# A graph network on one core: four small jobs move between VectorE, GpSimd and other places of their own queues

## The reference

```
h = relu(layernorm(x))
agg = segment_sum(h[src], dst)                      # layer 0: sums over edges
t = relu(batch_norm(((1 + eps) * h + agg) @ W1 + b1))
x = x + h + relu(batch_norm(t @ W2 + b2))

h = relu(layernorm(x))                              # layer 1: messages over edges
m = mish(mish([h[src], h[dst], edge_attr] @ W1 + b1) @ W2 + b2)
agg = segment_sum(m, dst)
u = mish([h, agg] @ W3 + b3)
y = h + u @ W4 + b4
x = x + layernorm(y) * gamma + beta
```

## Time and profile before

| quantity | value |
|---|---|
| time, median of 3 runs | 1142.65 us (1142.56 to 1143.2) |
| time of the profiled execution | 1142.65 us |
| its span, first to last instruction | 1140.8 us |
| mean granted TensorE clock | 0.953 |
| TensorE matmuls busy | 1061.1 us (93%) |
| VectorE, ScalarE, GpSimd busy | 875.8, 898.0, 676.5 us |
| chain that ended last | TensorE 85%, VectorE 10% |

### The profile page before, as it was taken

The page is one execution under the profiler, slowest core; times in us unless marked ns, Lnnn a source line. Parts: engine busy times, 40 slices in busy tenths (PEclk is TensorE's granted clock), DMA queues, the critical chain, the costliest instruction groups (busy, mean ns, idle before and its releaser), DMA issues.

```text
span 1140.8 us, 18418 instructions
## 1 busy us (share of the span) xinstructions
PE 1061.1 (93%) x5689; PEld 893.8 (78%) x5690; DVE 875.8 (77%) x1489; ACT 898.0 (79%) x1134; POOL 676.5 (59%) x589
## 2 busy tenths in 40 slices
PE   3565999998999999999999999999999999999897
PEld 1121889998788888888888888888888888888695
DVE  7798626544525388888899899989988888888786
ACT  6795745633621699999999999999999999999584
POOL 8696505000335487767788888888877677660217
PEclk7556999999899999999999999999999999999899
DMA  2000940110165477666676666666666666761002
GB/s 102 8 1 24 194 101 15 48 74 24 69 210 117 89 169 164 133 138 134 138 136 130 138 139 134 136 139 133 133 145 133 135 138 134 140 126 42 1 1 90
DMA packets 61087, 121.40 MB, mean 106 GB/s; under 512 B 7851, under 2 KB 18348, under 8 KB 60918
## 3 DMA queue, kind: packets, MB, share of 16 engines
q0 software_dynamic: 38048, 87.58, 38.9%
q1 hardware_dynamic: 22998, 33.32, 8.8%
HBM read 107.82 MB, written 7.80 MB: 101 GB/s over the span
## 4 chain that ended last, share of the span: by engine, by line
PE 85%; DVE 10%; issue 2%; POOL 1%; ACT 1%; DVEq 1%; ACTq 0%; POOLq 0%
PE banks L1032 12%; PE banks L1027 12%; PE banks L1028 12%; PE banks L932 10%; PE banks L1012 7%; PE banks L1049 6%; PE banks L1006 6%; PE banks L975 5%; PE banks L855 4%; PE banks L994 4%; DVE edge_counts L1682 3%; PE banks L1025 3%; DVE key_onehot L1638 2%; PE banks L1109 2%; PE banks L909 1%
## 5 line engine op out<-in xcount | busy, mean ns | idle before, releaser
L681 POOL DMA_INDIRECT gather_pq<-q_table,dst x157 | 295.6, 1883 | 56.9 <-issue 47.5
L673 POOL DMA_INDIRECT gather_pq<-p_table,src x157 | 173.0, 1102 | 137.2 <-PE banks L1012 84.0
L1027 PE MATMUL banks<-w_lo,h_hi 128*128 128x512 f32 x620 | 241.5, 389 | 0.0
L1028 PE MATMUL banks<-w_hi,h_hi 128*128 128x512 f32 x620 | 241.3, 389 | 0.0
L1032 PE MATMUL banks<-w_hi,h_lo 128*128 128x512 f32 x620 | 166.2, 390 | 0.0
L1028 PEld LDWEIGHTS banks<-w_hi,h_hi 128*128 128x128 f32 x620 | 116.4, 188 | 24.8
L1032 PEld LDWEIGHTS banks<-w_hi,h_lo 128*128 128x128 f32 x620 | 116.4, 188 | 24.2
L1958 DVE SCALAR_TENSOR_TENSOR h_full<-mish_work,banks 128x512 f32<-128x512 f32 (+1 forms) x154 | 98.5, 681 | 46.6 <-ACT mish_work L1336 43.9
L1027 PEld LDWEIGHTS banks<-w_lo,h_hi 128*128 128x128 f32 x620 | 116.5, 188 | 21.9
L1983 DVE SCALAR_TENSOR_TENSOR message<-mish_work,banks 128x1024 f32<-128x1024 f32 x78 | 95.3, 1222 | 8.7 <-ACT mish_work L1360 0.7
L1324 ACT ACTIVATE mish_work<-banks 128x1024 f32<-128x1024 f32 (+1 forms) x77 | 78.7, 1022 | 26.2 <-PE banks L1012 26.2
(11 more groups left out here) (266 smaller groups left out, 2720.2 us busy)
## 6 DMA issues: line engine op xcount, KB each, us to landing
edge_attr<-in_edge_attr_t SPq DMA_DIRECT2D x79, 128.0 KB, 3.6
x_nodes<-h_hi POOLq DMA_DIRECT2D x10, 256.0 KB, 12.4
x_nodes<-h_lo POOLq DMA_DIRECT2D x10, 256.0 KB, 7.9
p_table<-p_stage SPq DMA_DIRECT2D x10, 256.0 KB, 2.0
q_table<-agg_nodes SPq DMA_DIRECT2D x10, 256.0 KB, 2.9
gather_pq<-p_table,src POOLq DMA_INDIRECT x157, 3.9
gather_pq<-q_table,dst POOLq DMA_INDIRECT x157, 5.2
x_nodes<-in_x SPq DMA_DIRECT2D x3, 768.0 KB, 7.0
```

Source lines behind the costliest of these rows:

```text
L673: nc.gpsimd.indirect_dma_start(GP[:, 2 * j + k, :], None, p_tab[:, :], bass.IndirectOffsetOnAxis(ap=SRC[:, 2 * s + k:2 * s + k + 1], axis= ...
L681: nc.gpsimd.indirect_dma_start(GP[:, 2 * j + k, :], None, q_tab[:, :], bass.IndirectOffsetOnAxis(ap=DST[:, 2 * s + k:2 * s + k + 1], axis= ...
L1027: pe.matmul(at, h_high(s, j)[:, c, e], W2_LO[:, c, :], start=False, stop=False)
L1028: pe.matmul(at, h_high(s, j)[:, c, e], W2_HI[:, c, :], start=False, stop=False)
```

## The change

Four jobs are placed otherwise. What is computed stays as it was.

1. `AGG` is set to zero by VectorE, between step 2 and step 3 of the edge loop, and no longer by GpSimd.
2. The one-hot matrices of the last two steps are made by VectorE, behind `lo2(FINAL - 2)`. The semaphore `last_hots` goes, and `segment1` has no wait of its own for them.
3. In the second layer norm `ln_scale` of group 0 is moved behind the `residual` of group 1, the low part of tile 0 behind all statistics, and `std_2(2)` on ScalarE one tile earlier.
4. The bias rows are added into `X` and `H` tile by tile, right behind each Q tile, without the wait for the W3 split.

```
@@ gpsimd, gathers
             for s in range(SLOTS, EDGE_PAIRS):
                 gather_p(s)
                 gather_q(s - 1)
-                if s == SLOTS + 1:
-                    pool.wait_ge(h_lo, 2)
-                    pool.wait_ge(z2_done, 1)
-                    nc.gpsimd.memset(AGG[:, :, :], 0.0).then_inc(agg_done, 1)
...
             gather_q(EDGE_PAIRS - 1)
-            pool.wait_ge(seg_done, FINAL - 2)
-            for k in range(2):
-                nc.gpsimd.tensor_scalar(ONEHOT[:, 1, k, :], IOTA[:, 0:P], REL_G[...], None,
-                                        ALU.is_equal).then_inc(last_hots, 1)
-            pool.wait_ge(z2_done, FINAL)
-            nc.gpsimd.tensor_scalar(FINAL_HOT, IOTA[:, 0:P], REL_G[...], None, ALU.is_equal).then_inc(last_hots, 1)
@@ tensor, segment1
-                if isinstance(s, int) and s >= FINAL - 1:
-                    pe.wait_ge(last_hots, 3 if final else 2)
@@ scalar, tiles of the second layer norm
-                    if nt == 1:
+                    if nt == 0:
                         std_2(2)
                     normalise_2(nt + 2)
@@ vector, second layer norm
             for q, (a, b) in enumerate(FILLS):
                 residual(KD - 1, q)
-                if q > 1:
+                if q > 0:
                     ln_scale(q - 1, VAR_LN2, FILLS)
-                if q == FN - 1:
-                    low_ht(0, 1)
...
-                if q == 0:
-                    ln_scale(0, VAR_LN2, FILLS)
             ln_scale(FN - 1, VAR_LN2, FILLS)
-            low_ht(1, 3)
+            low_ht(0, 3)
@@ vector, Q tiles
                 nc.vector.tensor_tensor(AGG[:, nt, :], Z2[...], ROWS[:, ROW_B1, :], ALU.add).then_inc(q_moved, 1)
-
-            dve.wait_ge(w3a_lo, KD)
-            for nt in range(NT):
                 nc.vector.tensor_tensor(X[:, nt, :], X[:, nt, :], ROWS[:, ROW_BETA, :], ALU.add).then_inc(rows_used, 1)
                 nc.vector.tensor_tensor(H[:, nt, :], H[:, nt, :], ROWS[:, ROW_B4, :], ALU.add).then_inc(rows_used, 1)
@@ vector, edge steps
             for s in range(3):
                 edge_step(s, s % 2, s // 2)
+            dve.wait_ge(h_lo, 2)
+            dve.wait_ge(z2_done, 1)
+            nc.vector.memset(AGG[:, :, :], 0.0).then_inc(agg_done, 1)
             edge_step(3, 1, 1)
...
             hi2(FINAL - 2)
             lo2(FINAL - 2)
+            hots1(FINAL - 1, 1)
+            dve.wait_ge(z2_done, FINAL)
+            make_hots([FINAL_HOT], REL_G, 2 * FINAL).then_inc(hot_ready, 1)
```

More of the change, by code:

```diff
@@ L375, in gnn_kernel @@
         hot_ready, seg_done, agg_done = sem("hot_ready"), sem("seg_done"), sem("agg_done")
-        last_hots = sem("last_hots")
         xhot_ready, xseg_done, xagg_done = sem("xhot_ready"), sem("xseg_done"), sem("xagg_done")
@@ L726, in _ @@
             gather_q(EDGE_PAIRS - 1)
-            pool.wait_ge(seg_done, FINAL - 2)
-            for k in range(2):
-                nc.gpsimd.tensor_scalar(ONEHOT[:, 1, k, :], IOTA[:, 0:P], REL_G[:, 2 * (FINAL - 1) + k:2 * (FINAL - 1) + k + 1], None,
-                                        ALU.is_equal).then_inc(last_hots, 1)
-            pool.wait_ge(z2_done, FINAL)
-            nc.gpsimd.tensor_scalar(FINAL_HOT, IOTA[:, 0:P], REL_G[:, 2 * FINAL:2 * FINAL + 1], None, ALU.is_equal).then_inc(last_hots, 1)
             pool.wait_ge(msg_lo, EDGE_PAIRS)
@@ L1886, in residual_early @@
                     chain[0] += NT
-            def low_ht(first, end):
-                for nt in range(first, end):
-                    move_lo_node(HT_LO, HT_HI, nt, TR_HT, ht_hi, ht_lo)
             batch_norm(T1, KD, CG2, CBE2, MM_2, VAR_BN2, between=residual_early)
@@ L1908, in _, with low_ht @@
                         ins.then_inc(var_ready, 1)
-                if q == 0:
-                    ln_scale(0, VAR_LN2, FILLS)
             ln_scale(FN - 1, VAR_LN2, FILLS)
-            low_ht(1, 3)
+            def low_ht(first, end):
+                for nt in range(first, end):
+                    move_lo_node(HT_LO, HT_HI, nt, TR_HT, ht_hi, ht_lo)
+            low_ht(0, 3)
             dve.wait_ge(split_in, 48)
```

## The result

The changed kernel takes 1154.38 us (median of 4 runs, 1152.37 to 1155.82), the one before 1142.77 beside it. The ratio is 1.0102, with a 95% interval of 1.0087 to 1.0117: 11.6 us slower. The forecast was 1145.9 in a range of 1143.4 to 1148.8. It had the direction right and missed the size by 8.5 us. Every comparison is made with runs of the kernel before on the same chip: their median was 1143.87 us for the first four experiments, 1142.26 for the gaps, the attributes first, the memset in pieces and the 16 matmuls, and 1143.57 for the one gap, the small adds, the mended kernel and the repeat of the changed one. Two executions far outside all others, one of the kernel with gaps (1548.52 us) and one of the kernel before beside it (5915.63 us), are left out of the ratios.

What follows compares the result with a forecast made beforehand. TensorE alone was taken to bound the edge loop, so edits act only where it waits. Layer norm 1.2, bias rows −1.8, memset 3.2 and one-hots 0.6 sum to +3.2 us: 1145.9 us, range 1143.4 to 1148.8.

Steps and rivals of the forecast that it cites:

- Edit 4, the bias rows: Q tiles and first z1: attributes' wait goes, gain 2.4, less 0.6 for one TensorE wait; −1.8 us, gain bounds 1.2 to 2.4.
- An add with both inputs in SBUF (0.60) and a GpSimd split (1.24) then alternate: Q tiles: engines take turns, two adds take up to 3.7 us per 2.72 us tile period; TensorE waits about 0.6 once.
- the bias rows disturb more than they save: Rival, Q tiles: every add waits for a full GpSimd instruction, TensorE waits about 2 us, edit 4 gives nothing; 1147.9 us; 8%.
- Edit 1, the memset: Between steps 2 and 3: memset takes 4.8 us, beyond 1.63 us idle TensorE waits; +3.2 us, bounds +1.2 and +3.8.
- the rival that had 15%: Step 4: clock falls after TensorE idles 3.4 us ahead of z1(4), half-clock stretch costs 2.8 more; 1148.7 us; 15%.
- Edit 3, the layer norm: Start of P: low part of tile 0, and P with it, 1.6 us later; +1.2 us, middle of +0.8 to +1.6.
- The lower bound: Start of P: clock returns at the same moment, half-clock stretch 1.6 shorter gives back 0.8; +0.8 us.
- Edit 2, the last one-hots: Last sums: three one-hot matrices on VectorE's chain ahead of the last but one message; +0.6 us.
- the lower bound of the term: Last sums: smallest cost given for the last one-hots on VectorE; +0.4 us, upper bound +0.7.
- case of the fast memset: Rival, between steps 2 and 3: memset takes 2.8 us at 0.53 ns an element, costs 1.2; 1143.8 us; 18%.
- its third sign: Between steps 2 and 3: prediction is wrong if VectorE's memset row is under 4 us.
- The idle 2.06 at 366 did not bring it down: First z1: TensorE's 2.06 us wait left the clock up; said within the rival that the clock falls at step 4.

Runs made afterwards that it cites:

- the first four experiments: Each edit alone on the kernel before: bias rows 1146.79 us, memset 1148.97, last one-hots 1143.30, layer norm 1143.99.
- the gaps: Kernel before plus the bias-row edit, each of GpSimd's eight W3 split instructions waiting for the one before it to finish; 1140.21 us, ratio 0.9975.
- the attributes first: Kernel before with the attributes' work for z1(0) and z1(1) on VectorE moved ahead of the twenty bias-row adds; 1140.78 us, ratio 0.9983.
- the memset in pieces: Kernel before with the AGG memset on VectorE in three pieces ahead of edge step 2; 1143.07 us, ratio 1.0004.
- the 16 matmuls: Kernel before plus the memset edit, with 16 matmuls that feed nothing on TensorE ahead of z1(4); 1146.87 us, ratio 1.0035.
- the one gap: Kernel before plus the bias-row edit, GpSimd's first W3 split waiting for the last of four casts; 1141.33 us, ratio 0.9979.
- the small adds: Kernel before plus the bias-row edit, with eight two-column VectorE adds ahead of the X add of node tile 5; profiled execution alone, no time given.
- the mended kernel: Kernel before with all four edits, a gap after every GpSimd W3 split instruction and the memset in three pieces ahead of step 2; 1141.85 us, ratio 0.9988.
- the repeat of the changed one: The changed kernel with all four edits, run again against the kernel before on the same chip; 1152.96 us, ratio 1.0088.

## Why the prediction was wrong, step by step

**Edit 4, the bias rows: the step that failed.** "An add with both inputs in SBUF (0.60) and a GpSimd split (1.24) then alternate" was taken from a layer-norm row in which a small instruction got in behind the third of four splits. Here one add was held for the whole run of eight, in all four profiles of kernels with this chain without a gap (7.83, 7.82 and 7.84 us, and 7.43 in the repeat of the changed kernel). TensorE waited 4.38 in place of 0.6, and lost 2.8 more to the clock, which the prediction had not allowed for here at all. Against this stands the −2.64 of the attributes' wait, where 2.06 to 2.38 had been taken. Net +4.56 instead of −1.8, which is 6.4 of the 8.0 us missed in the profiled executions (11.2 less 3.2). Edit 1 is 2.0 of the rest, the end of the loop 1.0; 0.3 is spread over other rows of the table, and the layer norm and what lies ahead of the edits take 1.6 off again. With gaps the lag of two engines in turn is as replayed or less: TensorE waits 0.4 us with one gap and not at all with one behind every instruction, against the 0.6. The rule of the Trainium skill that the prediction cited (SBUF — State Buffer, "Who interferes with whom") is borne out in its kind, full blocking; what one block costs doesn't follow from it, and the trace gives it. The rival "the bias rows disturb more than they save" was the right one, with 8% and a price half of what came: it set the wait at 2 us, since it too let every instruction pass after one of the other engine.

**Edit 1, the memset: the mechanism was right, the size off.** The memset took 4.33 us (4.8 taken, from the short memsets; 0.85 ns an element, where the earlier trace rows gave 0.81 to 0.92). The row doesn't bear out the estimate of 5.3 us that the prediction worked out from the Trainium skill (VectorE: DVE Perf Modes, "Zero memsets can be issued as uint32 (trn2)"). Ahead of it stood 1.01 us of issue that no term had (1.02 with this edit alone); what they are, no run here tests. Both together add 3.63 to VectorE (3.2 forecast), and TensorE's wait of 3.82 is close to the 3.4 named. But the clock fell behind it, for 1.60 more: the rival that had 15%, at somewhat over half of its 2.8. The two weren't exclusive; the clock belonged into the term, since the prediction itself had TensorE idle for over 3 us. The 16 matmuls show that part by themselves.

**Edit 3, the layer norm: right in kind.** P's start moved by 1.22 against the residual, where 1.6 was replayed. The clock was back at 1.00 in the whole microsecond from 296 (0.51 in the earlier trace rows), so P ran at the lower level for about 4.1 us instead of 5.5, and that gave back 0.67. So +0.55 against +1.2. The lower bound had this mechanism, half of the delay given back; the middle between the bounds was the wrong choice. The way from the first residual to the first Q add, which holds all of this, took 43.37 us in the changed kernel, 43.38 with the edit alone, 43.37 in the mended one and 44.40 in the repeat, and 41.48 to 42.93 in the ten profiles without the edit. The edit costs something in all of them, but an execution's own clock moves the sum by as much as the edit does.

**Edit 2, the last one-hots: right in kind.** The wait ahead of the last but one sum is 2.51 or 2.52 us in all four profiles with the edit, where it was 2.13: 0.4, the lower bound of the term, for the 0.6 forecast. The 0.58 of the table, read ahead of the first transposes, hits 0.6 by luck, since the idle time there is 1.78 to 2.49 us without the edit too. The 1.01 that follows in the transposes (24 of them 5.36 us against 4.38) is the clock's, as the profiles of single edits show. By its time alone, the edit can't be told from nothing.

**The rest.** The loop was as forecast: TensorE busy 600.00 of the 600 us from 440 on, and no wait of TensorE for a gather from 300 to 1060 us. The prediction's lower end of 1143.4 isn't its own case of the fast memset, which it puts at 1143.8. Its case of a disturbed edit 4 that gives nothing should stand at 1147.7 (1145.9 plus 1.8) and not 1147.9. Neither changes the outcome. What was said would prove the prediction wrong (a wait among the Q tiles above 1 us, a clock below 1.0 after 410) is what did; the memset row under 4 us, its third sign, didn't come.

## What to carry to other kernels

Before work with two SBUF inputs goes beside a run of GpSimd instructions, count how long that run is without a pause, and allow for one instruction being held for all of it; a single wait inside the run took the hold away here. A wait of some microseconds that TensorE gets can have a second part in the clock: it had one behind every wait of 3.8 and 4.4 us in these profiles, and in three of the six profiles that have a wait of 2.1 to 2.6 for the attributes. Read the granted clock behind each. And where a move is meant to free one consumer, move only what that consumer needs: here the attributes ahead of the twenty adds were worth 1.9 us, and moving the adds themselves, beside a run without a pause, cost 2.6.

## What the runs showed of the hardware that was not expected

The longest hold was 7.84 us for an instruction of 0.68, behind eight of GpSimd. With one gap in the run VectorE got in one instruction ahead of the gap, and the engines alternated to the end of the run, at 1.09 to 1.78 us for an add of two SBUF operands.

The times of the kernel before range over 4.8 us within the first comparison (1141.28 to 1146.09) and over 5.3 in the other two. Part of this can come from the wait for the attributes. In the kernel with the memset alone and in the one with the 16 matmuls it was equally long, 2.58 us. Stretches behind it, first of the one with the memset alone, then of the other:

```profile
367.00:369.00 2.00, 2.00 (x16) 2.00 (x15) 0.00 (x0) 1.29 (x3) 1.69 (x2) 1.00 0.85 185
```

```profile
367.00:369.00 2.00, 2.00 (x12) 2.00 (x11) 0.00 (x0) 0.00 (x0) 0.16 (x1) 0.50 0.81 170
369.00:371.00 2.00, 2.00 (x9) 2.00 (x9) 0.00 (x0) 1.02 (x1) 1.27 (x2) 0.50 0.85 172
371.00:373.00 2.00, 2.00 (x11) 2.00 (x11) 0.00 (x0) 0.67 (x2) 1.70 (x2) 0.64 0.71 180
```

The same wait brought the clock down in one execution and not in the other. From the attributes' product to `z1(1)` the first took 12.00 us (365.00 to 377.00) and the second 14.81 (366.22 to 381.03), so the fall cost 2.8. Over all six profiles with this wait the clock stayed at 1.00 behind 2.06, 2.52 and 2.58 us and fell behind 2.40, 2.47 and 2.58. "The idle 2.06 at 366 did not bring it down", in the prediction, was true of that execution alone. That the wait is what spreads the times isn't shown: kernels without it range over 2.3 us (the bias rows alone) and 2.4 (the attributes first), but also over 3.8 (gaps, 11 runs) and 5.1 (the changed kernel again, 6 runs). Only profiled executions show where the clock falls, and each kernel has one.
